# Mixture-of-experts routing moved one turn later, with the gate carried in the scattered row

## The reference

```python
scores = softmax(xt @ Wr)                       # xt: 8192 x 128, layer-normed; 8 experts
topk_w, topk_idx = top_k(scores, 2)
topk_w = topk_w / (topk_w.sum(-1) + 1e-20)
out_all[e] = (silu(xt @ Wg[e]) * (xt @ Wu[e])) @ Wd[e]
out = sum over the 2 chosen experts of topk_w * out_all
x = x + out + (silu(xt @ Sg) * (xt @ Su)) @ Sd   # shared expert
```

## Time and profile before

| what | us |
|---|---|
| runs | 3187.52, 3190.71, 3202.62 |
| median | 3190.71 |
| profiled execution, its own time | 3181.02 |
| its span | 3179.0 |
| mean granted TensorE clock | 0.888 |
| busy TensorE / VectorE / ScalarE / GpSimd | 2622.8 / 2036.4 / 1808.9 / 853.9 |

### The profile page before, as it was taken

How to read it: one execution, slowest core, us unless ns; L and a number is a source line. 1 busy time by engine, 2 the same in 40 slices (tenths; PEclk the granted TensorE clock), 3 DMA queues, 4 the chain that set the end, 5 groups by cost and what they waited for, 6 DMA issues and landing times.

```text
span 3179.0 us, 76627 instructions
## 1 busy us (share of the span) xinstructions
PE 2622.8 (83%) x26192; PEld 2124.4 (67%) x26193; DVE 2036.4 (64%) x5025; ACT 1808.9 (57%) x4422; POOL 853.9 (27%) x1042
## 2 busy tenths in 40 slices
PE   3999898988989997986886289999999978958882
PEld 2777777777777776775765166667666657857671
DVE  2777666776766765874554666666766647855555
ACT  2777777777777775552444265555665545534441
POOL 0000000000000002663555232342442315744551
PEclk9999999999999997666999599899999876669996
DMA  6323323332332221111222200000000001112225
GB/s 147 48 42 45 48 41 51 49 46 42 49 44 41 41 41 36 40 43 54 69 68 71 88 2 2 2 2 2 2 2 2 2 2 35 41 46 68 70 69 171
DMA packets 117817, 140.22 MB, mean 44 GB/s; under 512 B 21324, under 2 KB 79825, under 8 KB 117360
## 3 DMA queue, kind: packets, MB, share of 16 engines
q1 hardware_dynamic: 100592, 101.63, 17.2%
q0 software_dynamic: 16896, 34.12, 3.2%
HBM read 45.85 MB, written 40.54 MB: 27 GB/s over the span
## 4 chain that ended last, share of the span: by engine, by line
PE 50%; DVE 18%; issue 12%; ACT 9%; another core or an unknown queue 5%; DMA 2%; SPq 1%; DVEq 1%; POOL 1%; ACTq 0%; POOLq 0%
PE psum L457 5%; PE psum L426 5%; PE psum L492 4%; ACT probs L446 3%; PE psum L1515 3%; DVE state L1718 3%; DVE neg_max L435 2%; PE psum L1563 2%; DVE x_sb L1288 2%; PE psum L543 2%; PE psum L1137 2%; PE psum L1432 2%; PE psum L1125 2%; PE psum L304 2%
## 5 line engine op out<-in xcount | busy, mean ns | idle before, releaser
L446 ACT ACTIVATE probs<-psum,neg_max 128x512 f32<-128x512 f32 (+3 forms) x1024 | 539.8, 538 | 244.3 <-DVE neg_max L435 243.5
L435 DVE TENSOR_REDUCE neg_max<-psum 128x1 f32<-128x512 f32 (+3 forms) x1024 | 457.3, 483 | 54.0 <-PE psum L427 24.9
L426 PE MATMUL psum<-ls,qs 96*128 96x512 f32 (+3 forms) x1024 | 380.9, 397 | 112.4 <-ACT probs L446 96.5
L457 PE MATMUL psum<-ident,probs 128*128 128x128 f32 x2560 | 428.4, 283 | 2.9 <-ACT probs L446 0.8
L1250 POOL DMA_INDIRECT y_tok<-yb,xb x272 | 267.7, 984 | 301.5 <-DVE yb L1225 226.6
L426 PEld LDWEIGHTS psum<-ls,qs 96*128 96x128 f32 x1024 | 198.2, 194 | 216.8 <-ACT probs L446 158.4
L325 POOL TENSOR_TENSOR rstd<-var_eps,half_neg 128x4 f32<-128x4 f32 x32 | 40.1, 1254 | 1103.1 <-DVE var_eps L321 1103.1
L476 DVE COPY probs_t<-psum 128x512 f32<-128x512 f32 (+1 forms) x384 | 230.4, 600 | 147.5 <-PE psum L457 140.4
L457 PEld LDWEIGHTS psum<-ident,probs 128*128 128x128 f32 x2560 | 273.7, 144 | 26.1 <-ACT probs_t L472 10.1
L914 POOL DMA_INDIRECT x_slot<-pay,pos_i x256 | 256.3, 1001 | 129.8 <-issue 76.1
L427 PE MATMUL psum<-causal_r,ident_r 128*128 128x128 f32 x1024 | 235.4, 242 | 0.0
(11 more groups left out here) (320 smaller groups left out, 6748.8 us busy)
## 6 DMA issues: line engine op xcount, KB each, us to landing
qs<-q_h SPq DMA_DIRECT2D x128, 256.0 KB, 5.5
xb<-x_slot SPq DMA_DIRECT2D x272, 66.0 KB
qs<-q_l SPq DMA_DIRECT2D x64, 256.0 KB, 5.7
y<-y_tok SPq DMA_DIRECT2D x32, 512.0 KB, 3.5
y_tok<-yb,xb POOLq DMA_INDIRECT x272
x_sb<-in_x SPq DMA_DIRECT2D x16, 256.0 KB, 5.5
x_slot<-pay,pos_i POOLq DMA_INDIRECT x256
out<-x_sb SPq DMA_DIRECT2D x16, 256.0 KB, 2.9
```

The costliest lines, as they stand in the source:

```text
L426: pe.matmul(o[:, at:at + n], q, ls[par][0:3 * LD, 0:n], start=(at == 0), stop=False, skip_group_check=True)
L435: last = dve.tensor_reduce(neg_max[:, par, h, qt:qt + 1], bank[u % 3][:, at:at + (qt + 1) * P], AX.X, ALU.max, negate=True)
L446: last = act.activation(probs[:, u % 3, c], bank[u % 3][:, c], ACT.Exp, bias=neg_max[:, par, h, qt:qt + 1], accum_out=row_sum[:, par, h, q ...
L457: last = pe.transpose(bank[3 + u % 2][:, c:c + P], probs[:, u % 3, c:c + P], ident[:, :])
```

## The change

- In turn b, places, gates and scatter belong to sequence b-1; those of sequence 15 follow the last turn. VectorE starts its turn with `place_vector(b-1)`, and `gates_vector(b-1)` stands before `route_b_vector(b)`.
- `shared_down_tensor(b-1)` moves on TensorE from the end of the turn to right behind the up products; `place_tensor(b)` becomes the last piece.
- The gate goes into column 129 of the row in `pay`, and the scatter waits for `gated` in place of `pos_done`. The tile `gates` is gone.
- `gated_up` becomes two instructions of 256 columns: (up * gate) * silu, with the gate a scalar per row read from `xb`.
- The combine is a plain sum: two additions of 512 columns a turn in place of eight multiply-adds of 128.
- On ScalarE the copy of the row (L793) and the high split of b+2 (L783) come earlier in the turn.
- The step counts that the waits compare with are recomputed for the new order.

```diff
         def scatter_gpsimd(pool, f, b, slot):
-            pool.wait_ge(z["pos_done"], f * SEQS + b + 1)
+            pool.wait_ge(z["gated"], f * SEQS + b + 1)
...
         def gates_vector
-            dve.tensor_tensor(gates[:, bass.ds(b * QT, QT), :].rearrange("p t k -> p k t"), gate2[:, :, :],
+            dve.tensor_tensor(pay[slot][:, :, :, D + 1].rearrange("p t k -> p k t"), gate2[:, :, :],
...
         def gated_up
-                dve.tensor_tensor(bh[par][:, :, :], psum[:, 2 * par:2 * par + 2, F:2 * F], bs[par][:, :, :],
-                                  ALU.mult).then_inc(z["gu_mul"], 1)
+                for k in range(2):
+                    last = dve.scalar_tensor_tensor(out=bh[par][:, k, :], in0=bank[2 * par + k][:, F:2 * F],
+                                                    scalar=xb[:, j, k, D + 1:D + 2], in1=bs[par][:, k, :],
+                                                    op0=ALU.mult, op1=ALU.mult)
+                last.then_inc(z["gu_mul"], 1)
...
         combine_vector, mix
-                    for t in range(QT):
-                        xt = tile_x(b * QT + t)
-                        gate = gates[:, bass.ds(b * QT + t, 1), k:k + 1].rearrange("p o k -> p (o k)")
-                        last = dve.scalar_tensor_tensor(out=xt, in0=y2[par][:, t, k, :], scalar=gate, in1=xt,
-                                                        op0=ALU.mult, op1=ALU.add)
-                    last.then_inc(z["mixed" if k else "mixed_a"], 1)
+                    xv = x_sb[:, bass.ds(b * QT, QT), :]
+                    dve.tensor_tensor(xv, y2[par][:, :, k, :], xv, ALU.add).then_inc(z["mixed" if k else "mixed_a"], 1)
...
         ffn_tensor, batch
+                if has_before(b):
+                    shared_down_tensor(pe, f, b - 1)
                 if left:
                     logits_tensor(pe, f, b + 1, 1 - par)
                 if left > 1:
                     route_turn_tensor(pe, f, b + 2, (slot + 2) % PAY_RING)
                 place_tensor(pe, f, b)
-                if has_before(b):
-                    shared_down_tensor(pe, f, b - 1)
...
         ffn_scalar, batch
+                    route_copy_scalar(act, f, b + 2, (slot + 2) % PAY_RING)
                 for k in range(FC):
                     shared_silu_scalar(act, f, b, k)
+                if left > 1:
+                    route_hi_scalar(act, f, b + 2, par)
                 for k in range(FC):
                     shared_hi_scalar(act, f, b, k)
-                if left > 1:
-                    route_hi_scalar(act, f, b + 2, par)
-                    route_copy_scalar(act, f, b + 2, (slot + 2) % PAY_RING)
...
         ffn_vector, batch
+                if has_before(b):
+                    place_vector(dve, f, b - 1, (slot - 1) % PAY_RING)
                 route_a_vector(dve, f, b)
...
+                if has_before(b):
+                    gates_vector(dve, f, b - 1, (slot - 1) % PAY_RING)
                 route_b_vector(dve, f, b)
...
-                place_vector(dve, f, b, slot)
-                gates_vector(dve, f, b)
                 if has_before(b):
                     shared_add_vector(dve, f, b - 1)
...
         ffn_gpsimd, batch
                     route_rstd_gpsimd(pool, f, b + 3, 1 - par)
-                scatter_gpsimd(pool, f, b, slot)
+                if has_before(b):
+                    scatter_gpsimd(pool, f, b - 1, (slot - 1) % PAY_RING)
```

More of the change, by code:

```diff
@@ L163, in program @@
         idall = sb("idall", [P, SEQS * QT, TOPK], I32)
-        gates = sb("gates", [P, SEQS * QT, TOPK])
         tab = sb("tab", [1, 2, BLOCKS], I32)
@@ L715, in tile_x, with steps_before, scored @@
             return x_sb[:, bass.ds(t, 1), :].rearrange("p o d -> p (o d)")
+        FIRST_STEPS = 11
+        def steps_before(f, b):
+            if isinstance(b, int) and b == 0:
+                return f * SEQS * R_STEPS
+            return f * SEQS * R_STEPS + (b - 1) * R_STEPS + FIRST_STEPS
+        def scored(f, b):
+            return steps_before(f, b) + (2 if isinstance(b, int) and b == 0 else 4)
         def route_pairs(eng, batch):
@@ L798, in logits_tensor @@
             if not (isinstance(b, int) and b == 0):
-                pe.wait_ge(z["r_step"], (f * SEQS + b - 1) * R_STEPS + 2)
+                pe.wait_ge(z["r_step"], scored(f, b - 1))
             for t in range(QT):
@@ L806, in route_scalar @@
             z = fs
-            act.wait_ge(z["r_step"], (f * SEQS + b) * R_STEPS + 2)
+            act.wait_ge(z["r_step"], scored(f, b))
             act.activation(r_exp[:, :, :], r_log[:, :, :], ACT.Exp).then_inc(z["r_exped"], 1)
@@ L812, in route_a_vector @@
             logits = bank[6][:, 0:QT * E].rearrange("p (t e) -> p t e", t=QT)
-            n = (f * SEQS + b) * R_STEPS
+            n = scored(f, b) - 2
             dve.wait_ge(z["log_mm"], f * SEQS + b + 1)
@@ L822, in route_b_vector @@
             z = fs
-            n = (f * SEQS + b) * R_STEPS
+            n = steps_before(f, b) + (0 if isinstance(b, int) and b == 0 else 7)
             dve.wait_ge(z["r_exped"], f * SEQS + b + 1)
@@ L854, in route_b_vector, with gates_vector @@
                                      op0=ALU.is_lt, op1=ALU.subtract).then_inc(z["r_step"], 1)
-        def gates_vector(dve, f, b):
+        def gates_vector(dve, f, b, slot):
             z = fs
-            n = (f * SEQS + b) * R_STEPS
+            n = steps_before(f, b + 1) + (2 if isinstance(b, int) and b == SEQS - 1 else 4) - 13
             dve.tensor_tensor(picked[:, :, :, :], pick[:, :, :, :],
@@ L878, in place_tensor @@
             if not (isinstance(b, int) and b == 0):
-                pe.wait_ge(z["r_step"], (f * SEQS + b - 1) * R_STEPS + 13)
+                pe.wait_ge(z["r_step"], steps_before(f, b) + 2)
             flat = chosen[:, :, :].rearrange("p t e -> p (t e)")
@@ L891, in place_vector @@
             z = fs
-            n = (f * SEQS + b) * R_STEPS
+            n = steps_before(f, b + 1) - 11
             dve.wait_ge(z["pos_mm"], f * SEQS + b + 1)
@@ L1208, in turned_in, with gated_up @@
                 dve.tensor_tensor(xt_l[par][:, :], bank[4][:, 0:2 * P], xt_h[par][:, :], ALU.subtract).then_inc(z["xt_lo"], 1)
-            def gated_up(p, par):
+            def gated_up(p, par, j):
                 dve.wait_ge(z["gu_silu"], f * N_PAIR + p + 1)
@@ L1232, in body @@
                 if in_range(st):
-                    gated_up(st, j % 2)
+                    gated_up(st, j % 2, j)
                 if in_range(st - 1):
@@ L1364, in ffn_vector @@
             route_pairs(dve, batch)
+            place_vector(dve, f, SEQS - 1, (SEQS - 1) % PAY_RING)
+            gates_vector(dve, f, SEQS - 1, (SEQS - 1) % PAY_RING)
             table_vector(dve, f)
@@ L1394, in ffn_gpsimd @@
             route_pairs(pool, batch)
+            scatter_gpsimd(pool, f, SEQS - 1, (SEQS - 1) % PAY_RING)
             moe_gpsimd(pool, f)
```

## The result

The changed kernel takes 3288.65 us (median of 4 runs) where the kernel before takes 3196.66 beside it: a ratio of 1.029, 95% interval 1.026 to 1.032. I had forecast 3130 us and a gain. The profiled execution took 3291.28 us, its span is 3289.4: 110 us more than the span before.

What follows compares the result with a forecast made beforehand. TensorE's 12.36 us was taken to bound the routing turn. Turns -31, end of routing -9, combine -33 and experts +12 gave -61 on 3181.0, hence 3120; the median was forecast at 3130 us, range 3095 to 3186.

Steps and rivals of the forecast that it cites:

- The routing turn: Routing: four laps bound a turn, the largest 12.36 us; -1.03 us a turn, -31 us over both stages.
- Rival 4: Routing: the count's signal waits for the scatter in flight, lap 20.8 us, total 3383 us; chance 0.05.
- the count's late signal: Routing: the signal of TensorE's last place matmul reaches VectorE some 4.5 us late.
- TensorE's 12.36 us as a floor: Routing turn: TensorE's work at granted clock 0.63 takes 12.36 us and was taken as the new turn.
- The end of routing: After the last turn: half of 18.7 us waiting for sequence 14's down product saved, -9 us, between 0 and -19.
- The table: After routing: last scatter hidden by 20 us of table writing if it starts within 8 us of the first step.
- The combine: Combine: two sums of 512 columns replace eight multiply-adds, -19 us first stage, -14 second, together -33 us.
- The experts: Expert stage: two 256-column products replace one of 512, +0.18 us a pair, exposed in half of 136: +12 us.
- ScalarE's and TensorE's moves: Routing turn: the earlier ScalarE pieces and TensorE's moved down product were costed at 0.
- The range: Total time: from 3095 to 3186 us.
- rival 3: Whole kernel: turn reaches 11.7 us, end signals in time, new product free, -103 us, 3088 us; chance 0.11.

Runs made afterwards that it cites:

- the second group: Follow-up runs on one chip, where the kernel before took 3053 us and the unedited changed kernel 1.0493 of it.
- the orders alone: Kernel before with only TensorE's down product of b-1 ahead of the logits and ScalarE's earlier copy and split: 0.9942 of before.
- the gate went into the row alone: Kernel before with gate in the scattered row, new product and new combine, places and scatter in their old turn: 0.9944 of before.
- the ring of eight: Changed kernel with eight payload tiles instead of four: 0.9926 of before.
- the third group: Follow-up runs on another single chip, where the kernel before took 3189 us.
- the gate in the row with the two orders: Kernel before with gate in the scattered row and the new TensorE and ScalarE orders, places and scatter in their old turn: 0.9894 of before.
- the first group: Follow-up runs on one chip, where the kernel before took 3050 us.
- the control of the first group: Kernel before with eight payload tiles instead of four: 0.9997 of before.
- the ring of eight with the old orders: Changed kernel with eight payload tiles and the old orders on TensorE and ScalarE: 0.9899 of before.

## Why the prediction was wrong

- **The step that failed** is the list of laps under "The routing turn". For GpSimd it says that "what it can still wait for is the statistics ahead of rstd", and for VectorE it takes "the turn less its idling". It is silent on the payload ring. The wait at L755 had no row in the profile, because b-2's scatter was two turns old. The change takes one turn out of a slack that the code shows and the profile doesn't. In place of -31 us: +64 us in each stage from the first row maximum to the last but one, with some twelve turns at 19.1 in place of 13.3.
- **Rival 4** had the right shape (rstd waits for the statistics, the scatter stands behind rstd) and almost the lap, 20.8 us. It hung it on the wrong wait, the count's late signal, and so got too small a chance; that its lap is near the measured 19.1 is luck. The signal is no longer in the way: no row of L905 ends in "remote" in the profile after.
- **TensorE's 12.36 us as a floor** was wrong too. The 63 matmuls of the new turn take 10.04 us. The granted clock over the turn is the same, 0.64 against 0.63, but that is a mean over work and idling, and work now falls on its fast part. These are the down product before, then the down product of the new turn, the idling behind TensorE's logits, and the work from the transposes on, columns as in rows 2:

```profile
1336.18:1341.34 5.16, 5.16 (x31) 5.16 (x27) 2.96 (x14) 0.67 (x2) 3.80 (x4) 0.50 0.16 52
```

```profile
1391.89:1394.57 2.68, 2.68 (x24) 2.68 (x25) 1.62 (x8) 0.35 (x2) 2.07 (x3) 1.00 0.12 39
1396.10:1403.87 7.77, 0.00 (x1) 0.01 (x1) 1.80 (x12) 1.67 (x5) 3.22 (x4) 0.57 0.10 35
1403.87:1410.30 6.43, 5.12 (x24) 3.96 (x25) 6.14 (x21) 5.07 (x8) 2.07 (x2) 0.50 0.00 0
```

  The down product alone is 2.5 us shorter, at 2.4 GHz in place of 1.2. Busy time is a floor only at the clock that this work gets.
- **The end of routing** was forecast at -9, for a late signal that might be freed. From the last row maximum to the table's first step there are indeed 10.0 us in both stages, where they were 16.1 and 21.1. But the late signal is not gone, it has moved into the turn before, where VectorE's sum now waits 9.80 us for the down product of sequence 13 (9.69 in the second stage):

```profile
1502.86 0.69 DVE L989 TENSOR_TENSOR x_sb<-psum,x_sb 128x512 f32<-128x512 f32 x1 [9.80 <-remote]
```

  That turn takes 19.3 us, and 9.3 in the second group, where no signal is late. Taken together, from the last but one maximum to the table, it is 29.4 us before and after in the first stage and 34.3 to 29.2 in the second: -5.
- **The table** was costed at nothing, "hidden by it as long as it starts within 8 us". The last scatter was in time, some 4 us after the first step, and yet the stretches grew from 20.8 to 28.2 and from 16.6 to 27.6 us. The scatters and SyncE's eight padding writes now run at the same time, and the writes take 17.8 us (last section). On the second group's chip the same kernel's writes take 8.1 us; there the last scatter starts 6.0 us after the first step, SyncE's first load follows the last indirect DMA by 3.8 us, and the stretch is 21.7, where the orders alone have 17.5. So "within 8 us" was wrong as well.
- **The combine**: -33 forecast, -17.5 and -16.7 measured as stretches. The first one's loads had room. In the second the stores set the end, as the prediction says: from its first sum to the end of the kernel it is 51.1 us before and 39.2 after, -12. So it is -29.

```profile
3246.77 24.60 SPq L1282 DMA_DIRECT2D y<-y_tok  x16
3271.90 14.68 SPq L2153 DMA_DIRECT2D out<-x_sb  x16
```

- **The experts**: the new product takes what I took from the nearer row, 0.473 a piece, against 0.479 here:

```profile
L1226 DVE SCALAR_TENSOR_TENSOR bh<-psum,xb,bs 128x256 f32<-128x256 f32 x272 | 119.1, 479 | 121.6 <-ACT bs L1187 82.6
```

  Over both stages the change is +0.5 us on the chip of the prediction, +7 where the gate went into the row alone, and +18 with the ring of eight, each against its control. The forecast of +12 lies between; how many of the pairs are exposed differs by case, and no run shows why. The Trainium skill says that this instruction runs at half rate with both sources in SBUF and not bf16 ("Vector Engine (DVE) Microarchitecture Reference", Points that are easy to get wrong). The trace agrees: with a source in PSUM, 128 more columns cost 140 ns (L1728's 339 to 479 here), 1.1 ns a column, while two of L1701 in a row, with both in SBUF, start 0.54 us apart for 256 columns, 2.1 ns a column.
- **ScalarE's and TensorE's moves**, taken as 0 in the turn, are worth 18 us by themselves in the second group, and nothing that shows in routing and table in the third.
- **The range**: its lower end, 3095, is not "halfway to rival 3", which would be 3109. Nothing hangs on it.

By terms, then: the end of routing, the combine and the experts came to -5, -29 and about 0, -34 in all where -30 was forecast, so this part's sum is right although its terms are not. The turn and the table, forecast at -31 and 0, came to about +128 and +18.

## What to carry to other kernels

A change that delays a step by one turn takes one turn from every ring of buffers between that step and the reuse of its tiles. Count them from the code: for each buffer, in which turn it is given back and in which it is asked for, before and after. A wait that costs nothing has no row. Then look at what is queued behind such a wait on its engine: here the wait at the head of VectorE's turn held what its own releaser needed, and so a wait that looked one transfer long closed a ring of 19 us. And shortening the turn below one engine's total only moves the rest behind the loop: add up the stage and its tail. The same goes for a late signal that leaves one stretch: look where it has gone.

## What the runs showed of the hardware

**Late signals, on some chips.** In the profiles of the kernel before and after, and in all three of the third group, TensorE's results are noticed late in the ffn stages. These are waits of the kernel before over the whole span, and then of the gate in the row with the two orders:

```profile
ACT y_half L1188 <- remote: 52.9, 43, 2.4
ACT hid_h L952 <- remote: 47.2, 4, 16.1
DVE pos L894 <- remote: 45.3, 24, 3.3
```

```profile
ACT x_pad L782 <- remote: 120.3, 26, 5.6
DVE pos L894 <- remote: 69.2, 27, 3.9
```

No profile of the first and the second group, eight in all, has a row that ends in "remote". In the attention and state space stages, where GpSimd issues no indirect DMA, no signal is late in any of these profiles. The same goes for SyncE. Its eight padding writes and the register work between them, in the kernel before beside one indirect DMA and beside none; in the changed kernel beside ten; in the ring of eight, in the first group, beside seven:

```profile
1454.70 10.39 SPq L1030 DMA_DIRECT2D x_slot<-padt  x8
2842.45 7.98 SPq L1030 DMA_DIRECT2D x_slot<-padt  x8
```

```profile
1517.92 17.78 SPq L1041 DMA_DIRECT2D x_slot<-padt  x8
```

```profile
1413.96 8.18 SPq L1050 DMA_DIRECT2D x_slot<-padt  x8
```

So in some executions an engine's signals and small instructions come late while indirect DMAs are being issued, and this fits the 4.5% that separate 3050 from 3190 us for the same kernel: between the profile before (3179.0 us) and the control of the first group (3035.1), 62 of the 144 us lie in routing and table, 75 in the experts. But it is not so in every stage: in the ring of eight with the old orders, in the third group, the second routing stage has no "remote" row, and the writes take 9.5 us beside seven indirect DMAs and 8.3 beside six. That the indirect DMAs cause it I have only from where it occurs: no run took them away or added them elsewhere, and what differs, the chip or something else, stays open.

**TensorE's clock.** The new turn leaves TensorE idle for 9.1 of 19.14 us, and the granted clock is 0.64, a mixture of 1.2 and 2.4 GHz as before at 92% busy (0.63). By the rows under TensorE's floor above, it is 1.00 while the down product and the logits run; it has fallen within the 7.8 us of idling behind them, and the work from the transposes on starts at 0.50. By the Trainium skill, "TensorE: Matmul & The Clock Gate" (Why this matters for your kernels), long idle gaps make the clock fall; the trace agrees in this. The rule did not bear on the turn of the kernel before: TensorE is never idle for more than 0.52 us in it, and yet its clock is 0.50 for most of the turn. Why is not shown. On the first group's chip the ring of eight has 0.80 in routing at 84% busy and its control 0.71 at 87%.
